# A selective-scan layer whose steps are taken in pairs, with one convolution tap moved to ScalarE and GpSimd

## The reference

```python
zxbcdt = u @ in_proj_w.T
xBC = causal_conv1d(xBC, conv_w, conv_b)      # 4 taps along the tokens, per channel
cum = jnp.cumsum(-softplus(dt), axis=2)
seg = jnp.exp(cum[:, :, :, None, :] - cum[:, :, None, :, :])
cb = jnp.einsum('bcihn,bcjhn->bcijh', Cr, Br)
scores = jnp.where(mask, seg * cb, 0.0)
y_intra = jnp.einsum('bcijh,bcjhp->bcihp', scores, xr)
```

## Time and profile before

| | us |
|---|---|
| median of three runs | 1249.69 |
| lowest and highest of them | 1248.21, 1578.18 |
| profiled execution | 1247.24 |
| its span in the profile | 1245.5 |
| TensorE busy in the span | 1081.7 (87%) |
| VectorE busy | 848.7 (68%) |
| ScalarE busy | 518.3 (42%) |
| GpSimd busy | 251.2 (20%) |

### The profile page before, as it was taken

How to read it: one execution, slowest core, us unless ns; L and a number is a source line. 1 busy time by engine, 2 the same in 40 slices (tenths; PEclk the granted TensorE clock), 3 DMA queues, 4 the chain that set the end, 5 groups by cost and what they waited for, 6 DMA issues and landing times.

```text
span 1245.5 us, 19789 instructions
## 1 busy us (share of the span) xinstructions
PE 1081.7 (87%) x7172; PEld 664.1 (53%) x7192; DVE 848.7 (68%) x1816; ACT 518.3 (42%) x1125; POOL 251.2 (20%) x522
## 2 busy tenths in 40 slices
PE   3999897789999998888999998898998998886567
PEld 1444554554444666554444666554445666565346
DVE  4999625468999646469998646479997545566126
ACT  2766520335666211336666212246665213221224
POOL 3222101132222011032221101132221001221632
PEclk9999898899999999899999999899999999898779
DMA  5789300002433000003442001004346404015646
GB/s 184 274 268 288 91 0 18 1 2 88 138 118 118 1 1 18 18 2 116 124 126 95 1 1 34 1 2 147 119 124 168 90 1 119 2 31 147 193 168 205
DMA packets 74258, 113.33 MB, mean 91 GB/s; under 512 B 5944, under 2 KB 64192, under 8 KB 73266
## 3 DMA queue, kind: packets, MB, share of 16 engines
q1 hardware_dynamic: 70322, 100.08, 26.1%
q10 hardware_dynamic: 2304, 8.39, 2.1%
q0 software_dynamic: 1536, 3.60, 1.0%
HBM read 93.38 MB, written 19.27 MB: 90 GB/s over the span
## 4 chain that ended last, share of the span: by engine, by line
PE 62%; DVE 21%; issue 7%; ACT 5%; POOL 2%; DMA 2%; DVEq 0%; POOLq 0%; SPq 0%; ACTq 0%
PE bank L897 23%; DVE hf L1684 6%; PE bank L962 5%; DVE nmax L2099 3%; PE bank L1048 3%; PE bank L1064 3%; PE bank L1183 3%; PE bank L1140 2%; PE bank L1229 2%; DVE u L1916 2%; PE bank L1226 2%; PE bank L910 2%; PE bank L977 2%; PE bank L1213 1%; PE bank L888 1%
## 5 line engine op out<-in xcount | busy, mean ns | idle before, releaser
L897 PE MATMUL bank<-uT,w_in 128*128 128x512 f32 (+1 forms) x584 | 284.0, 613 | 16.7 <-DVE hf L1684 10.9
L1684 DVE SCALAR_TENSOR_TENSOR hf<-bank,conv_w,hf 128x510 f32<-128x510 f32 (+2 forms) x384 | 277.5, 743 | 16.0 <-ACT hf L1390 10.9
L897 PEld LDWEIGHTS bank<-uT,w_in 128*128 128x128 f32 (+1 forms) x584 | 99.7, 187 | 113.3 <-issue 78.5
L1390 ACT ACTIVATE hf<-bank,conv_b,conv_w 128x512 f32<-128x512 f32 x128 | 99.4, 777 | 135.0 <-PE bank L897 135.0
L2099 DVE TENSOR_REDUCE nmax<-bank 128x2 f32<-128x256 f32 (+1 forms) x128 | 65.4, 553 | 74.6 <-PE bank L1229 74.6
L1529 POOL TENSOR_TENSOR rs<-ve,half 128x2 f32<-128x2 f32 x56 | 39.0, 697 | 324.7 <-DVE ve L1816 324.7
L1048 PE MATMUL bank<-hf 64*128 64x256 f32 x512 | 91.0, 432 | 12.6 <-issue 7.2
L897 PE MATMUL bank<-uT,w_gu 128*128 128x512 f32 x224 | 99.0, 593 | 0.0
L1048 PEld LDWEIGHTS bank<-hf 64*128 64x128 f32 x512 | 39.5, 187 | 70.1 <-issue 63.8
L1370 ACT ACTIVATE xc<-bank 128x512 f32<-128x512 f32 x44 | 26.3, 597 | 114.6 <-PE bank L897 77.1
L1916 DVE TENSOR_TENSOR turned_p<-dec,bank 128x768 f32<-128x768 f32 x64 | 60.9, 952 | 16.3 <-PE bank L1049 5.5
(11 more groups left out here) (317 smaller groups left out, 2147.5 us busy)
## 6 DMA issues: line engine op xcount, KB each, us to landing
hf<-cum_dram SPq DMA_DIRECT2D x32, 384.0 KB, 3.6
dec<-cum_dram SPq DMA_DIRECT2D x32, 384.0 KB, 3.6
tmp<-cum_dram SPq DMA_DIRECT2D x32, 384.0 KB, 3.6
x<-cum_dram SPq DMA_DIRECT2D x32, 384.0 KB, 3.6
y_dram<-xf SPq DMA_DIRECT2D x16, 512.0 KB
hf<-y_dram ACTq DMA_DIRECT2D x16, 512.0 KB, 4.1
w_in<-in_w_in SPq DMA_DIRECT2D x1, 3584.0 KB, 11.7
w_in<-in_w_egu SPq DMA_DIRECT2D x6, 512.0 KB, 10.0
```

Of the source, the lines that this page charges most:

```text
L897: mm = pe.matmul(plan[key][0:n, :], w[:, k, cols], uT[:, k, :], start=k == 0, stop=k == DC - 1)
L1390: act.activation(dst, plan[key][:, :], ACT.Identity, bias=conv_b[:, j:j + 1], scale=conv_w[:, j, TAPS - 1:TAPS]).then_inc(tap0.sem, 1)
L1684: ins = dve.scalar_tensor_tensor(d, x, conv_w[:, j, TAPS - 1 - s:TAPS - s], d, ALU.mult, ALU.add)
```

## The change

TensorE's loop goes over pairs instead of steps: both steps' products, then both projections of pair p+2, then, behind an odd pair, y for both its steps. The last two pairs keep their order by sequence. VectorE does the three taps of a chunk w=0 together behind the second mask multiply of a pair, and the taps of the chunk w=1 at the start of the next pair, ahead of its mask multiplies. From pair 2 on, the last tap of the chunk w=1 is not VectorE's any more: ScalarE writes the product of the shifted bank and the tap's weight into a free SBUF tile (`last_product`, one buffer, so it waits until GpSimd has added the one before), VectorE waits for that product, does taps 1 and 2 and drains the bank with tap 2, and GpSimd adds the product to the chunk, behind its masks of step 2p+1. TensorE waits for that sum (`conv_sum`) before the products of the pair.

```diff
+        last_product = yg[:, 1, :].rearrange("p (b l) -> p b l", b=SEQS)[:, :, TAPS - 1:SEQ]
...
+        tap3 = signal("tap3", PAIRS - 2)
+        conv_sum = signal("conv_sum", PAIRS - 2)
@@ TensorE
-                for g in range(2 * PAIRS):
+                def states_times_queries(g):
                     p, b = steps[g]
-                    ns = (2 * g, 2 * g + 1)
-                    if b == 0:
-                        for w in range(2):
-                            pe.wait_ge(*plan.drained(("BC", p, w), r))
                     pe.wait_ge(*plan.before(("CB", p, b), r))
-                    for second in [products(n) for n in ns]:
+                    for second in [products(n) for n in (2 * g, 2 * g + 1)]:
                         mm = second()
                     mm.then_inc(plan.fills(("CB", p, b)), 1)
+
+                for p in range(PAIRS):
+                    for w in range(2):
+                        if p < PAIRS - 1:
+                            pe.wait_ge(*plan.drained(("BC", p, w), r))
+                            if w == 1 and p >= 2:
+                                pe.wait_ge(conv_sum.sem, conv_sum.at(r, p - 1))
                     if p + 2 < PAIRS:
-                        if p + 2 == PROJ_PAIRS[1] and b == 0:
+                        for b in range(2):
+                            states_times_queries(2 * p + b)
+                        if p + 2 == PROJ_PAIRS[1]:
                             pe.wait_ge(w_proj[2], 16)
-                        project_bc(p + 2, b)
-                    if g == 1:
+                        for w in range(2):
+                            project_bc(p + 2, w)
+                        if p % 2 == 1:
+                            for b in range(2):
+                                add_y(p, b)
+                    else:
+                        b = p - (PAIRS - 2)
+                        for i in range(2):
+                            g = 2 * (PAIRS - 2) + 2 * b + i
+                            if b == 0 and i == 1:
+                                for w in range(2):
+                                    pe.wait_ge(*plan.drained(("BC", PAIRS - 1, w), r))
+                                pe.wait_ge(conv_sum.sem, conv_sum.at(r, PAIRS - 2))
+                            states_times_queries(g)
+                            if b == 1 and i == 0:
+                                add_y(*steps[g - 1])
+                    if p == 0:
...
-                    if g >= 1 and steps[g - 1][0] % 2 == 1:
-                        add_y(*steps[g - 1])
@@ ScalarE
+                def tap_product(p):
+
+                    key = ("BC", p, 1)
+                    if p > 2:
+                        act.wait_ge(conv_sum.sem, conv_sum.at(r, p - 2))
+                    x = plan[key][:, :].rearrange("p (b l) -> p b l", b=SEQS)[:, :, 0:SEQ - TAPS + 1]
+                    act.activation(last_product, x, ACT.Copy, scale=conv_w[:, 18 + p, 0:1]).then_inc(tap3.sem, 1)
...
                     if p + 2 < PAIRS:
                         first_tap(("BC", p + 2, b), bc[:, (p + 2) % 3, b, :], 2 + 16 * b + p + 2)
+                        if b == 1:
+                            tap_product(p + 2)
@@ GpSimd
+                    p = g // 2
+                    if g % 2 == 1 and p >= 2:
+
+                        pool.wait_ge(tap3.sem, tap3.at(r, p - 1))
+                        pool.wait_ge(*plan.drained(("BC", p, 1), r))
+                        settle(pool)
+                        x = bc[:, p % 3, 1, :].rearrange("p (b l) -> p b l", b=SEQS)[:, :, TAPS - 1:SEQ]
+                        pool.tensor_tensor(x, x, last_product, ALU.add).then_inc(conv_sum.sem, 1)
@@ VectorE
+            def tap_and_drain(r, s, key, dst, j):
+
+                dve.wait_ge(chain, last_tap[0])
+                d = dst.rearrange("p (b l) -> p b l", b=SEQS)[:, :, s:SEQ]
+                x = plan[key][:, :].rearrange("p (b l) -> p b l", b=SEQS)[:, :, 0:SEQ - s]
+                dve.scalar_tensor_tensor(d, x, conv_w[:, j, TAPS - 1 - s:TAPS - s], d, ALU.mult, ALU.add)\
+                    .then_inc(plan.drains(key), 1)
...
+                def all_taps(p, w):
+                    if w == 1:
+                        dve.wait_ge(tap3.sem, tap3.at(r, p - 1))
+                        tap(r, 1, [bc_chunk(p, w)], taps_done)
+                        tap_and_drain(r, 2, *bc_chunk(p, w))
+                        return
+                    for s in range(1, TAPS):
+                        tap(r, s, [bc_chunk(p, w)], taps_done)
...
                     p, b = steps[g]
+                    d = 2 * g % 4
+                    if g % 2 == 0 and 1 <= g // 2 <= PAIRS - 2:
+                        all_taps(g // 2 + 1, 1)
...
                     if g == 0:
                         tap(r, TAPS - 1, [bc_chunk(1, w) for w in range(2)], taps_done)
-                    if g >= 1 and (g - 1) // SEQS + 2 < PAIRS:
-                        tap(r, 2, [bc_chunk((g - 1) // SEQS + 2, (g - 1) % SEQS)], taps_done)
-                        tap(r, 3, [bc_chunk((g - 1) // SEQS + 2, (g - 1) % SEQS)], taps_done)
-                    if p + 2 < PAIRS:
-                        tap(r, 1, [bc_chunk(p + 2, b)], taps_done)
+                    if g % 2 == 1 and g // 2 + 2 < PAIRS:
+                        all_taps(g // 2 + 2, 0)
```

More of the change, by code:

```diff
@@ L1914, in _ @@
                         dve.wait_ge(y_added.sem, y_added.at(r, 8 * (p4 // 2) + 4 * b4 + 2 * (p4 % 2) + 2))
-                    d = 2 * g % 4
                     dve.tensor_tensor(sc[g % 4], dec[:, d:d + 2, :], both_cb[g % 2][:, :, 0:TRI],
```

## The result

The changed kernel took 1221.51 us (median of four runs, 1220.88 to 1222.5), the kernel before 1250.49 beside it: a ratio of 0.977, 95% interval 0.976 to 0.979. One run of the kernel before was in a slow state, 1578.18 us; the ratio is of the others, whose median is 1249.69. The forecast was 1236 in a range of 1229 to 1249, so the direction was right and the gain twice what was forecast, 28 us instead of 14. It is also more than the 20.7 us of idle time that I had called the most a change could win.

The account below looks back on a forecast made before the run. TensorE bounds the kernel (87% busy), losing 0.39 us per period to VectorE. Start 1.0, periods 2.3, rest 0.1 give 3.4 us per round, 13.6 in all: 1247.24 to 1233.6, plus 2.45 for the median: 1236 us, range 1229 to 1249.

Parts of the forecast that it names:

- the 20.7 us of idle time: TensorE's idle time over the four scans, claimed as the most a change that leaves TensorE its work could win.
- TensorE's work per period, 12.66 us: Two pairs (four steps) of a scan: projections, products and y additions sum to 12.66 us, claimed as the new period.
- the start: Start of a scan, up to the products of pair 2: 1.0 us won per round.
- the output block: Two output instructions inserted at step 20: claimed to fall into a loose half of the period.
- the tail: End of a scan: products of step 29 start at 400.5 instead of 403.91, behind GpSimd's add of 1.23 us.
- the 0.1 for the rest: Per round, 0.1 us won: what the old order lost around the inserted block, less the longer tail.
- The waits inside the period: Steps 4 to 27: the 0.39 us each period loses to VectorE goes, six times, 2.3 us per round.
- VectorE's relief: 14 taps per round leave VectorE, 0.70 us off each pair's 5.92; claimed worth nothing alone, since TensorE has 12.66.
- The wait comes back: Rival: ScalarE's decay before the second chunk's first tap starts 0.5 late, even pairs lose their gain; 1245 to 1250, chance 0.18.
- GpSimd and VectorE did not exclude each other: Rival: GpSimd's add keeps VectorE from its masks, costing 2 to 8 us; 1238 to 1244, chance 0.08.
- No table load: Rival: a ScalarE table load at the product lengthens the second chunk's path; slower, 1301 us, chance 0.05.
- More is won: Rival: every idle of TensorE in the scan is won, 1229 by the 20.7 us; 1218 to 1230, chance 0.05.

Follow-up runs that it names:

- run 5: Changed kernel plus one 128-column matmul, weights on 64 rows, between the products of a pair's two steps; 1227.98 us, ratio 0.982 to the kernel before.
- run 6: Changed kernel plus one 128-column matmul, weights on all 128 rows, between the products of a pair's two steps; 1248.33 us, ratio 0.999 to the kernel before.
- run 7: Changed kernel with an odd pair's second-sequence y additions moved behind the next pair's products; 1235.66 us, ratio 0.981, beside 1233.02 for the changed kernel.
- run 2: Kernel before with only the tap moved (ScalarE product, GpSimd add), TensorE and VectorE in the old step order; 1257.70 us, ratio 1.000.
- run 1: Kernel before with the new orders of TensorE and VectorE, but the last tap kept on VectorE; 1247.18 us, ratio 0.990.

## Why the prediction was wrong, point by point

- **TensorE's work per period, 12.66 us: wrong, and the main miss.** The step that failed is the sum 4 x 1.92 + 4 x 0.85 + 2 x 0.79 (four projections J, four steps' products C, two y additions Y). Its prices were read off the old order and used for the new one in "Nothing is late, so the period is 12.66". The new period is 11.89 with nothing late either. C = 0.85 holds only behind another kind of work; behind its own kind it is 0.65, and Y and J shrink too. Five changes of shape fewer per period brought TensorE's busy time from 12.72 to 11.89; runs 5, 6 and 7 show a price of 0.14 to 0.20 us for one. The bound of 20.7 us failed with it: it holds for a change that leaves TensorE its work, and this one did not. The Trainium skill (TensorEngine Tiling (Array Packing), "Key Properties") says that a change of the tiling mode drains TensorE. It gives no price; these runs agree with it in that each change costs time, but none of them tells a drain from a weight load that is not hidden.
- **How the 6.9 us a round come about, against 3.4.** The six periods gave 6 x 0.77 = 4.6 us more than forecast and the start 0.1 to 0.2; the output block and the tail, below, took back 0.6 each, and the 0.1 for the rest did not come. That makes about 6.9.
- **The waits inside the period: right.** The forecast 0.39 us per period was won; the chain holds no VectorE from 310.67 on, until the inserted output block.
- **The start: nearly right.** From the first mask multiply to the products of pair 2 it took 10.5 us with both y additions, against 10.9 with one: 1.1 to 1.2 us won, forecast 1.0. It also contains shorter y additions.
- **The inserted output block: wrong sign.** I had it in a loose half. The period is now shorter, so the halves are tighter: two periods around it take 374.42 - 350.04 = 24.38, 0.6 more than 23.78. The forecast had put a small gain there.
- **The tail: forecast 0.6 us too short.** GpSimd's add was sized right (1.265 for 1.23). The hand-overs were not: the add started 0.17 behind the tap and TensorE 0.26 behind the add, and the last mask before the add ended just when the tap did. The last projection ended at 386.3 and the tap 3.4 behind it, forecast 3.1. Products of step 29 came 5.0 us after the last projection, forecast 4.45.
- **VectorE's relief: right that it alone is worth nothing,** and in the old order for the reason given: run 2 has TensorE busy 12.70. In the new order that reason is gone. There the relief is needed, because TensorE's shorter period falls below what VectorE needs with all taps (11.84 by the forecast's pitches, 12.06 busy in run 1). Without it 12.34, with it 11.89. The gain is an interaction: order 1.0%, move 0.0%, both 2.3% in the whole time, and 15.3, 1.0 and 27.3 us in the scans. VectorE's busy time fell by 35.5 us instead of 40; no run shows why.
- **The rivals.** "The wait comes back" did not happen in the even pairs' windows for which it was forecast. GpSimd and VectorE did not exclude each other: the mask multiplies kept 943 to 955 ns with 56 adds beside them. No table load appeared at the product. "More is won" comes nearest, with a chance of 0.05, but by another mechanism and with a bound that did not hold: TensorE kept 17.1 of its 20.7 us of idle time in the scans and got less work instead. None of the rivals had TensorE's work change.

## What to carry to other kernels

When a change reorders matmuls of different weight shapes, count the changes of shape in both orders before adding up prices, and read a price once behind its own kind and once behind another. Idle time is a ceiling for what better waiting can win, not for what a better order can. And order the engine that a batch feeds in the same batches: TensorE's batches alone made this kernel 1.7% slower.

## What the runs showed of the hardware

A change between 128 x 128, 64 x 128 and 128 x 32 float32 weights cost TensorE 0.12 to 0.20 us at a granted clock of 1.00. In the period of the changed kernel it is 0.20 before products, 0.14 before y and 0.12 before projections. One more change around y cost 0.14 (12.03 against 11.89). Between 64 and 128 rows four changes cost 0.81 (12.95 against 12.14), 0.20 each, or by the estimate above 0.15. Float32 matmuls with weights on different halves of the rows ran beside each other: the records of 344.43 and 344.44 in run 5 start 0.01 us apart.

A float32 add of 506 columns on GpSimd took 1.265 us, 1.7 times VectorE's multiply-add of 0.744, and VectorE's mask multiplies, which read one operand from a PSUM bank, kept 943 to 955 ns beside it.
